# A macaron block on one core: the order of the work at the borders between its three stages

## The reference

```python
def ffn(x):      # quantised; H = 256, F = 1024, groups of 128
    h = (x - mean(x)) * rsqrt(var(x) + EPS) * gamma + beta
    y = silu(h @ dequant(fc1_q, fc1_scales) + fc1_bias)
    return x + 0.5 * (y @ dequant(fc2_q, fc2_scales) + fc2_bias)

def mixer(x):    # N = 64; a scan over the 1024 steps of each sequence
    a, b, c, d = sigmoid(x @ Wa + ba), x @ Wb + bb, tanh(x @ Wc + bc), x @ Wd + bd
    s_t = a_t * s_(t-1) + (1 - a_t) * b_t
    return (c * s) @ Wy + by + d

x = x + 0.5 * ffn(layernorm(x))
x = x + mixer(layernorm(x))
x = x + 0.5 * ffn(layernorm(x))
```

## Time and profile before

| | us |
|---|---|
| median of the three timed executions | 703.87 |
| the profiled execution | 704.72 |
| its span, first to last instruction | 702.9 |
| PE busy | 673.6 (96%) |
| PE weight loads busy | 540.0 (77%) |
| ACT busy | 646.2 (92%) |
| DVE busy | 641.5 (91%) |
| POOL busy | 599.2 (85%) |

### The profile page before, as it was taken

The page is one execution under the profiler, slowest core; times in us unless marked ns, Lnnn a source line. Parts: engine busy times, 40 slices in busy tenths (PEclk is TensorE's granted clock), DMA queues, the critical chain, the costliest instruction groups (busy, mean ns, idle before and its releaser), DMA issues. The chain is left out here.

```text
span 702.9 us, 13646 instructions
## 1 busy us (share of the span) xinstructions
PE 673.6 (96%) x3222; PEld 540.0 (77%) x3222; DVE 641.5 (91%) x1326; ACT 646.2 (92%) x1084; POOL 599.2 (85%) x673
## 2 busy tenths in 40 slices
PE   4999999999999999889999989999999999999997
PEld 3668888888888878667777867678888888888885
DVE  6699999999999999599999995999999999999887
ACT  4989999999999999588888887989999999999994
POOL 4799999999999999646666686989999999999974
PEclk9999999999999999999999999999999999999999
DMA  7660000000000000000000000000011000000001
GB/s 251 184 214 1 1 0 0 0 0 0 0 0 0 1 1 1 1 1 0 0 0 0 1 0 1 0 31 32 30 48 42 30 30 30 30 31 31 31 31 62
DMA packets 19963, 20.22 MB, mean 29 GB/s; under 512 B 1565, under 2 KB 19667, under 8 KB 19923
## 3 DMA queue, kind: packets, MB, share of 16 engines
q1 hardware_dynamic: 19824, 19.74, 8.7%
q10 hardware_dynamic: 98, 0.02, 0.0%
HBM read 11.37 MB, written 8.39 MB: 28 GB/s over the span
## 5 line engine op out<-in xcount | busy, mean ns | idle before, releaser
L390 POOL TENSOR_TENSOR g_lo<-g_full,g_hi 128x512 fp32r<-128x512 f32 x256 | 331.4, 1295 | 31.1 <-ACT g_hi L561 28.5
L701 DVE SCALAR_TENSOR_TENSOR z_acc<-ps_z,cols,z_acc 128x512 f32<-128x512 f32 x448 | 321.6, 743 | 28.4 <-PE ps_z L928 19.2
L928 PE MATMUL ps_fc<-h_hi,q_sb 128*128 128x512 f32 x512 | 213.3, 417 | 3.1 <-ACT ps_fc L544 2.8
L928 PE MATMUL ps_z<-g_hi,q_sb 128*128 128x512 f32 x512 | 202.5, 395 | 0.3
L559 ACT ACTIVATE g_full<-ps_fc,safe_scale 128x512 f32<-128x512 f32 x256 | 194.2, 759 | 8.8 <-PE ps_fc L928 6.7
L928 PE MATMUL ps_fc<-h_lo,q_sb 128*128 128x512 f32 x512 | 202.2, 395 | 0.0
L928 PE MATMUL ps_z<-g_lo,q_sb 128*128 128x512 f32 x512 | 200.9, 392 | 0.0
L561 ACT ACTIVATE g_hi<-ps_fc,safe_scale 128x512 fp32r<-128x512 f32 x256 | 195.6, 764 | 0.0
L544 ACT ACTIVATE ps_fc<-ps_fc,bias,ratio 128x512 f32<-128x512 f32 x192 | 156.7, 817 | 3.7 <-PE ps_fc L928 1.9
L928 PEld LDWEIGHTS ps_z<-g_hi,q_sb 128*128 128x128 f32 x512 | 96.1, 188 | 26.2 <-DVE z_acc L701 3.1
L928 PEld LDWEIGHTS ps_fc<-h_hi,q_sb 128*128 128x128 f32 x512 | 97.3, 190 | 23.7 <-ACT ps_fc L544 3.4
(11 more groups left out here) (107 smaller groups left out, 816.8 us busy)
## 6 DMA issues: line engine op xcount, KB each, us to landing
resid<-in_L_attn_x SPq DMA_DIRECT2D x15, 512.0 KB, 4.5
out_x<-resid SPq DMA_DIRECT2D x15, 512.0 KB, 2.9
q_int<-in_L_ffn_fc_q SPq DMA_DIRECT2D x4, 512.0 KB, 7.6
resid<-in_L_attn_x SPq DMA_DIRECT2D x2, 256.0 KB, 2.9
out_x<-resid SPq DMA_DIRECT2D x2, 256.0 KB, 2.5
wd_sb<-in_L_attn_Wd SPq DMA_DIRECT2D x1, 256.0 KB
wy_raw<-in_L_attn_Wy SPq DMA_DIRECT2D x2, 64.0 KB
bias_rows<-in_L_attn_by SPq DMA_DIRECT2D x1, 128.0 KB
```

The lines of the kernel that those rows point to most:

```text
L390: nc.gpsimd.tensor_tensor(g_lo[:, g % 4, :], g_full[:, g % 4, :], g_hi[:, g % 4, :].bitcast(F32), ALU.subtract).then_inc(g_ready, 1)
L701: nc.vector.scalar_tensor_tensor(out=z, in0=bank_of(g, n, par), scalar=col(R_S2 + KC * g + n), in1=z, op0=ALU.mult, op1=ALU.add).then_inc( ...
L928: last = nc.tensor.matmul(out, w, v, start=start and i == 0, stop=stop and i == len(pairs) - 1, skip_group_check=not start)
```

## The change

Six edits, all in the order of work around the borders:

1. In the first tile of each feed-forward (`before` = 0), ACT scales the groups 1, 3, 5, 7 and DVE 0, 2, 4, 6. Before it was ACT 0, 1, 2, 3, 5, 7 and DVE 4, 6, as it stays in all other tiles.
2. In the second tile of each feed-forward the variance is computed in group 7 and not in group 4.
3. The drain of FF1: the turn of mixer tile 1's first half moves from group 0 to group 2, that of its second half from group 1 to behind the `ab` products of mixer tile 0. Both halves of the last `turn_back` come behind mixer tile 0's c products.
4. On ACT the first mixer tile's `normalise` (four blocks) moves from behind tanh to ahead of a and b.
5. In a mixer tile DVE fills the bias banks of tile t in tile t itself, behind its statistics and variance and ahead of its scan. Before it was done at the end of tile t - 1, ahead of those statistics.
6. At the mixer's end POOL does `cs_low` of tile 14 ahead of `residual` of tile 0, and `rsqrt` and `normalise` of FF2's tile 1 move ahead of `cs_low` of tile 15; ACT does its half of that `normalise` ahead of `cs_hi` of tile 15; and PE does the y products of tile 15 ahead of `add_products` of FF2's group 0.

```diff
-    SCALED_ON_ACT = (0, 1, 2, 3, 5, 7)
-    SCALED_ON_DVE = (4, 6)
+    SCALED_ON_ACT = ((1, 3, 5, 7), (0, 1, 2, 3, 5, 7))
+    SCALED_ON_DVE = ((0, 2, 4, 6), (4, 6))
...
-    VARIANCE_AT = 4
+    VARIANCE_AT = (7, 7, 4)
...
@@ cs_low (POOL)
-                if t == NT - 2:
-                    pool.wait_ge(resid_scaled, NT + 1)
-                elif t < NT - 2:
+                if t == NT - 1:
+                    pool.wait_ge(xhat_ready, 2 * NT + 2)
+                else:
                     pool.wait_ge(xn_ready, 2 * t + 4)
...
@@ feed_forward, tile (POOL)
-                        else:
+                        elif ff0 == 0:
                             rsqrt(ln0 + 1, 1, True)
-                        if not before and f == 1:
+                        if ff0 == 0 and not before and f == 1:
                             normalise(ln0 + 1, 1, 1, halves[0], True)
...
@@ mixer_tile (POOL)
-                if behind == 1:
-                    residual(t + (NT + 2), 0, 0)
+                if not behind:
+                    residual(2 * NT, 0, 0)
+                    rsqrt(2 * NT + 1, 1, True)
+                    normalise(2 * NT + 1, 1, 1, halves[0], True)
...
@@ mixer_tile (ACT)
+                if not before:
+                    normalise(t + (NT + 2), t + 2, par, range(SUB), xhat_ready)
                 act.wait_ge(ab_done, t + 1)
...
-                if behind:
+                if before and behind:
                     normalise(t + (NT + 2), 0 if behind == 1 else t + 2, par, range(SUB), xhat_ready)
-                else:
+                elif not behind:
                     nc.scalar.activation(silu_table[:, :], minus_half[:, 0, 0:1], ACT.Silu)
+                    normalise(2 * NT + 1, 1, 1, halves[1], xhat_half_ready)
...
@@ mixer_tile (DVE)
                     variance(t + (NT + 2), par, twice)
+                if before and behind:
+                    fill_bias(t, par)
                 if before:
                     scan(t, par)
...
-                if behind >= 2:
-                    fill_bias(t + 1, 1 - par)
...
@@ feed_forward, tile (PE)
+                        if ff0 and not before and f == 1:
+                            y_products(NT - 1, 1)
                         if f >= 1:
-                            add_products(ff, ln, f - 1, par)
+                            add_products(ff, ln, f - 1, par, ff0, min(before, 1))
...
-                        if ff0 and not before and f == 1:
-                            y_products(NT - 1, 1)
...
@@ the drain (PE)
                         d_products(0, 0, f)
-                        if f == 0:
-                            pe.wait_ge(ffn_added, 2 * NT - 2)
-                        turn(NT + 1, 1, f, shares=NT + 2)
+                    if ff0 == 0 and f == 2:
+                        pe.wait_ge(ffn_added, 2 * NT - 2)
+                        turn(NT + 1, 1, 0, shares=NT + 2)
...
@@ mixer_tile (PE)
                 products(ps_ab, ...).then_inc(ab_done, 1)
                 if not before:
-                    turn_back(NT - 1, 1, 0, 2 * NT + 4)
+                    turn(NT + 1, 1, 1, shares=NT + 2)
...
                 if not before:
-                    turn_back(NT - 1, 1, 1, 2 * NT + 4)
+                    for half in range(2):
+                        turn_back(NT - 1, 1, half, 2 * NT + 4)
                     return
```

More of the change, by code:

```diff
@@ L238, in wait, with scaled_count @@
                 eng.wait_ge(signal, count)
-        def scaled_count(ff, f, where):
-            return len(where) * ff + (where.index(f) + 1)
+        def scaled_count(ff, f, ff0, later, where):
+            openings = (1 if ff0 else 0) + later
+            return len(where[1]) * ff + ((len(where[0]) - len(where[1])) * openings + where[later].index(f) + 1)
         def bank_of(g, n, par):
@@ L540, in scale_half @@
                 act.wait_ge(half_done, FC * ff + (f + 1))
-                if type(ff) is int and ff == 0 and f == SCALED_ON_ACT[0]:
+                if type(ff) is int and ff == 0 and f == SCALED_ON_ACT[0][0]:
                     act.wait_ge(bias_ready, 1)
@@ L576, in tile @@
                     for f in range(FC):
-                        if f in SCALED_ON_ACT:
+                        if f in SCALED_ON_ACT[min(before, 1)]:
                             scale_half(ff, f)
@@ L677, in scale_half @@
                 dve.wait_ge(half_done, FC * ff + (f + 1))
-                if type(ff) is int and ff == 0 and f == SCALED_ON_DVE[0]:
+                if type(ff) is int and ff == 0 and f == SCALED_ON_DVE[0][0]:
                     dve.wait_ge(bias_ready, 1)
@@ L720, in tile @@
                             add_ffn(ff - 1, t - 1, ADD_AT[before].index(f))
-                        if f in SCALED_ON_DVE:
+                        if f in SCALED_ON_DVE[min(before, 1)]:
                             scale_half(ff, f)
@@ L730, in tile @@
                                 add_mixer(NT - 1, 1, half)
-                        if ff0 == 0 and not behind and f == VARIANCE_AT:
+                        if ff0 == 0 and not behind and f == VARIANCE_AT[2]:
                             lower_bias()
@@ L746, in tile @@
                             statistics(t + 3 if behind >= 3 else 2 - behind, statistics_at[f])
-                        if (behind >= 3 or ff0 == 0) and f == (VARIANCE_AT if before else FC - 1):
+                        if (behind >= 3 or ff0 == 0) and f == VARIANCE_AT[before]:
                             variance(ln + 3, 1 - par, behind >= 3)
@@ L940, in half_products, with add_products @@
                                                for w in q1_parts for h in (h_hi, h_lo)]).then_inc(half_done, 1)
-            def add_products(ff, ln, f, par):
+            def add_products(ff, ln, f, par, ff0, later):
                 if f == 0:
@@ L1020, in feed_forward @@
                     if f == 0:
-                        add_products(end - 1, ln0 + NT - 1, FC - 1, 1)
+                        add_products(end - 1, ln0 + NT - 1, FC - 1, 1, ff0, 1)
                     fc2(end - 1, FC + f - LAG, 1, 1)
```

8 lines of the change are left out of this document (4 added, 4 removed).

## The result

The changed kernel takes 720.08 us (median, 719.8 to 721.47) against 704.63 (703.81 to 705.78) for the kernel before on the same chip: a ratio of 1.0225, 95% interval 1.0212 to 1.0238. It is 15.5 us slower, where 3.6 less were forecast, and it lies outside the range. Its profiled span is 718.2, 15.3 longer than that of before, at a mean granted clock of 0.995.

What follows compares the result with a forecast made beforehand. PE bounds the kernel inside its stages, so only borders can gain. +0.3 - 1.1 + 2.5 + 0 - 4.2 - 1.1 = -3.6 from 704.72 gives 701.1 us, 700.3 on the median; range 697.5 to 703.7.

Steps and rivals of the forecast that it cites:

- The middle of the mixer: Mixer tiles: PE sets the pace at 8.11 us, DVE's 7.4 us tile has slack, so the term is 0.
- earlier statistics bring POOL's work forward, which frees those 0.6: Mixer tiles: DVE's `cs_full` takes 1.29 us, 0.68 where POOL is idle; POOL's earlier work would free the difference.
- The slower rival: Mixer tiles: the variance's last operations are held under POOL's `cs_low`, DVE's tile grows to 8.7 us; 706.9 us, chance 0.07.
- The mixer's start: The drain and first mixer tiles: late a and statistics before the fill delay tile 1's d products; +2.5 us, bounds +1.2 and +4.2.
- The 0.7 that was to come back: Mixer's start: 0.7 us of the +3.2 returns, as waits in the old second and third tile are then covered.
- The rival of the clock: Mixer's start: PE's clock falls behind waits of about 3 us, costing 1.7 us; 702.0 us, chance 0.19.
- The variance: Second tile of each feed-forward: 1.6 us of wait goes, 0.5 is given back in the third; -1.1 each in FF1 and FF2.
- The deadline: Group 7, second feed-forward tile: PE needs DVE's bank 1.3 us after an unheld variance, about 0.9 before a held one ends.
- The opening groups: FF1's first tile: group 0 on DVE costs 0.9 us, group 2 saves 0.66; +0.3, bounds -0.66 and +0.9.
- The mixer's end: Mixer's end and FF2's opening: earlier `add_products` -2.4 us, less ACT work -1.7, PE's c-product wait -0.15; -4.2, bounds -2.4 and -4.7.
- the moved `rsqrt`, `normalise` and the table load are done by 424, under DVE's sum, additions and `cs_full`: Mixer's end: this moved work hides under DVE's, so `cs_low` of tile 15 ends at 426.1 instead of 428.05.

Runs made afterwards that it cites:

- experiment 1: The changed kernel without edit 5, the fill back at the end of the tile before: 704.96 us against 704.09, ratio 1.0011.
- experiment 2: The kernel before with edit 5 alone, the fill moved into its own tile: 721.14 us, ratio 1.0242.
- experiment 3: The changed kernel with one added wait, so that POOL's two `xn_low` start only after DVE's scan: 711.22 us, ratio 1.0103.
- experiment 5: The kernel before with only `cs_low` of tile 14 moved ahead of `residual`: 702.23 us against 704.28, ratio 0.9965.
- experiment 10: The kernel before with `cs_low` of tile 14 ahead of `residual`, and FF2's tile 1 `rsqrt` ahead of the last `cs_low`: 701.11 us against 704.54, ratio 0.9951.
- experiment 4: The changed kernel with DVE's fill of the bias banks behind the scan instead of ahead of it: 737.89 us, ratio 1.0465.

## Why the prediction was wrong

**The middle of the mixer: 0 forecast, +13.7 measured. This step failed.** The prediction counted DVE's tile at 7.4 us and called the rest slack. The count was right: 9.25 less the 0.70 of `var_terms` (361.44 to 362.22, where before it was 0.08 to the next start) and less the 1.05 of the scan (2.25 from start to start, against 1.20) is 7.5. What failed is the sentence "earlier statistics bring POOL's work forward, which frees those 0.6". It asked only what POOL's work would leave, `cs_full`, and not where it would land. The variance releases `rsqrt`, and that the pair of `xn_low`; with the variance 1.13 (the fill) earlier, and the scan no earlier, the pair lands on the scan. The saving of 0.6 happened, and 1.75 came for it. Experiments 1 and 2 show that edit 5 alone makes this loss, and experiment 3 that the meeting with POOL does: with the pair kept off the scan the middle loses 2.4 and not 13.7. A row that stood in the text could have warned, though it settles nothing by itself: in the earlier trace rows DVE was busy 19.39 of 20 in the mixer. The slack under PE's 8.11 was there only if every hold disappeared.

**The slower rival** had the side and half of the place: the variance is held under `cs_low` in every tile, for 0.70 ("0.75 at most" was its own bound). By itself that makes 8.2 us and next to nothing, as it said. It missed the scan; its price of 706.9 was wrong by 13.

The Trainium skill (SBUF — State Buffer, Who interferes with whom) says that a DVE instruction with two SBUF inputs contends with a GpSimd instruction that reads SBUF. The scan has two such inputs, so the rule covers it, and experiments 1 to 3 agree (1.22 apart, 2.33 together). The prediction had put the rule without its conditions and applied it to the variance alone.

**The mixer's start: +2.5 forecast, +3.8 measured.** The chain was right step by step: `ab` at 292.57 (292.4 was said), `normalise` then table load ahead of a, a 2.2 later (1.8), `cs_full` 1.7 later (1.3), then statistics and variance for 2.1 (2.0), and the d products held by the fill, 3.8 later (3.2). The 0.7 that was to come back did so by 0.4, in the tile from `ab` of tile 2 (8.54 against 8.97), which is counted in the middle. The rival of the clock was right that it falls, behind a wait of 2.42, and wrong in its price: the fall lay under the wait for the fill and cost nothing. PE's new wait for the fill was 1.54 and not 3, since PE had waited for b before it. With either part alone a fall counts: edits 3 and 4 without the fill make the start 2.9 late (experiment 1), the fill without them 5.0, of which 2.9 are the d products at the lower clock (experiment 2). So the two lie over one another, and their costs don't add.

**The variance: -2.2 forecast.** Edit 2 alone gave 0.9. The deadline had been placed well: a variance held for 1.35 makes PE wait 0.82, where 0.9 was said. Of the two ends, held and not held, the prediction took a value nearer to not held; the prediction itself said that POOL is busy back to back in that group, and that should have decided.

**The opening groups: +0.3 in FF1** (its own terms, 0.9 less 0.66, make 0.24). Measured +0.4 (the turn of tile 1 at 39.76 against 39.36).

**The mixer's end: -4.2 forecast, -1.8 in the changed kernel (from `ab` of tile 15 to FF2's first turn 17.60 us against 19.38), -0.8 for edit 6 alone.** The two terms that were credited to `cs_low` of tile 14, the wait of 2.64 and the clock, did go: experiments 5 and 10 are 2.1 and 3.4 faster (their spans 3.1 and 4.0 shorter), by the move of `cs_low`(14) and then of `rsqrt` alone. The failed step is "the moved `rsqrt`, `normalise` and the table load are done by 424, under DVE's sum, additions and `cs_full`", which put the last `cs_low` at 1.95 earlier. `residual` took 3.59, not 2.60: it now lies beside DVE's whole scan and sum, where before it met only the scan's first 0.4 us (read from the overlap, not tried apart); `shift` came so late that ACT's `normalise` waited 1.18 for it, and `cs_hi` and `cs_low` queued behind. The last `cs_low` ended 1.0 earlier, PE stood 3.07 before y, and the clock fell there instead (0.50 from 444.5 to 447).

## What to carry to other kernels

Where a step moves on one engine, list every instruction of the others that its semaphore releases, and lay those over the neighbours on DVE and POOL: the length of an instruction in a trace is its length under the neighbours that it has there, and a hold that disappears in one place can return in a dearer one. Two edits that each hide in a wait can each use up the other's cover, so the pair must be summed as a pair. And a busy share of 19.39 of 20 on the second engine is not slack, even if some of it is waiting in disguise. Before work is reordered there, show from the rows that the holds go.

## What the runs showed of the hardware

- A scan of 64x512 with two SBUF inputs on DVE and a 128x512 `tensor_tensor` on POOL ran one behind the other when started together: 1.22 and 1.27 alone, 2.33 for the scan, and 2.19 for the next POOL instruction. Each engine pays.
- An operation of 128x4 on DVE took 0.17 alone, and 0.87 or 1.35, the rest of POOL's instruction, under one. In the earlier trace rows one took 1.79, under two POOL instructions in a row (one of 0.56 from 44.96, then `g_lo`).
- `residual` on POOL (four of 128x256) took 2.60 where DVE's variance, drive and the scan's start lay beside it, and 3.59 beside the whole scan and the sum; elsewhere one such block took 0.56. That the scan is the cause was read from the overlap and not tried apart.
- PE's granted clock fell to the 1.2 GHz level behind single waits of 2.42, 2.64 and 3.07 us, and stayed at 1.00 behind one of 1.54. The length of the wait alone doesn't tell: behind 3.08 in experiment 3 it stayed at 1.00, and in experiment 4, with a wait of 1.9 to 2.0 in most mixer tiles, it fell in two of them, where the d products took 5.4 instead of 3.7. First the row of experiment 3, then one of the two:

```profile
436.57 0.39 PE L1065 MATMUL ps_z<-wy_hi,cs_parts 128*128 128x256 f32 x1 [3.08 <-POOL cs_parts L437]
323.38 5.38 PE L1055 MATMUL ps_fc<-wd_sb,q_int 128*128 128x256 f32 x16 [1.94 <-DVE ps_fc L884]
```

- Executions of one kernel differ in this. Of the 59 executions of the kernel before in the experiments, 32 have a mean granted clock of 0.996 or 0.997 and a median of 704.9 us, 25 one of 0.999 and a median of 703.6. So a gain that rests on a fall that goes, here 1.7 us in the prediction's sum, is perhaps had in a part of the executions only. Which of the falls comes and goes can't be told from one profile of each kernel.
